# Gated cross-attention with a LoRA mixture: Q of all sixteen head pairs by block products, and two of the seven V products of the first two groups moved to the start

## What is computed

```python
x = _rmsnorm(hidden_states, ln_weight)          # hidden_states: layer norm of the input
h_q = (x @ w_q.T).reshape(b, lq, H, DH)
h_k = (key_value_states @ w_k.T).reshape(b, lk, H, DH)
h_v = (key_value_states @ w_v.T).reshape(b, lk, H, DH)
score = jnp.einsum('bqhd,bkhd->bhqk', h_q, h_k) + position_bias[None]
...
attn = jnp.einsum('bhqk,bkhd->bqhd', softmax(score), h_v).reshape(b, lq, H * DH)
return hidden_states + attn @ w_out.T
```

## Time and profile before

| | us |
|---|---|
| median of 3 runs (lowest, highest) | 823.38 (822.85, 823.48) |
| the profiled execution | 823.18 |
| its span, first to last instruction | 821.4 |
| TensorE busy | 814.2 |
| VectorE busy | 584.1 |
| GpSimd busy | 440.3 |
| ScalarE busy | 385.1 |

### The profile page before, as it was taken

One profiled execution on the slowest core, in us unless ns is written; L12 is line 12 of the kernel. 1 busy time (PEld: TensorE's weight loads), 2 busy tenths in 40 slices (PEclk: granted clock), 3 DMA queues, 4 the chain that ended last, 5 costly groups with the idle time before them and its releaser, 6 DMA issues.

```text
span 821.4 us, 14316 instructions
## 1 busy us (share of the span) xinstructions
PE 814.2 (99%) x4288; PEld 701.3 (85%) x4288; DVE 584.1 (71%) x1003; ACT 385.1 (47%) x1051; POOL 440.3 (54%) x410
## 2 busy tenths in 40 slices
PE   8999999999999999999999999999999999999998
PEld 7888888878888889888888888888888888888887
DVE  6985656767646354987779778877887788778752
ACT  5564444456241514566345634563456355545410
POOL 2366666580476372756764575457545754574200
PEclk9999999999999999999999999999999999999999
DMA  9347445543544555697566556655665565555002
GB/s 305 106 137 259 153 155 171 178 150 127 179 148 160 179 191 163 228 281 234 160 211 230 186 159 211 229 181 163 212 220 180 165 220 210 183 178 180 1 26 78
DMA packets 78991, 145.52 MB, mean 177 GB/s; under 512 B 7920, under 2 KB 45296, under 8 KB 77040
## 3 DMA queue, kind: packets, MB, share of 16 engines
q1 hardware_dynamic: 78960, 145.12, 52.6%
HBM read 94.77 MB, written 50.33 MB: 177 GB/s over the span
## 4 chain that ended last, share of the span: by engine, by line
PE 94%; DVE 2%; issue 1%; DMA 1%; SPq 1%; POOL 1%; ACT 1%; DVEq 0%; POOLq 0%
PE proj_ps L1962 17%; PE proj_ps L1768 15%; PE proj_ps L2018 12%; PE proj_ps L2037 8%; PE score_ps L1768 7%; PE proj_ps L1836 5%; PE score_ps L2037 5%; PE score_ps L1805 3%; PE pv_ps L2037 2%; PE turn_ps L2037 2%; PE proj_ps L2216 2%; PE pv_ps L2018 2%; PE turn_ps L2018 2%; PE turn_ps L1805 2%; PE pv_ps L1805 2%; PE score_ps L1836 2%
## 5 line engine op out<-in xcount | busy, mean ns | idle before, releaser
L618 POOL TENSOR_TENSOR comb<-mask_add,bias_sb 128x1024 f32<-128x1024 f32 x32 | 77.2, 2435 | 144.7 <-DVE attn L1515 144.7
L853 ACT ACTIVATE attn<-attn,neg_max 128x128 f32<-128x128 f32 x256 | 99.2, 391 | 37.4 <-DVE neg_max L1504 37.3
L1064 ACT ACTIVATE w_hi<-w_raw 128x256 fp32r<-128x256 f32 x105 | 39.9, 413 | 96.5 <-POOL w_raw L703 74.2
L713 POOL TENSOR_TENSOR w_lo<-w_raw,w_hi 128x256 fp32r<-128x256 f32 x105 | 74.4, 749 | 0.0
L1537 DVE TENSOR_TENSOR acc<-proj_ps,acc 128x512 f32<-128x512 f32 x70 | 48.3, 690 | 36.4 <-PE proj_ps L1768 36.4
L1768 PE MATMUL proj_ps<-w_hi,tf_hi 128*128 128x512 f32 x156 | 61.1, 391 | 0.0
L1768 PE MATMUL proj_ps<-w_lo,tf_hi 128*128 128x512 f32 x156 | 60.7, 389 | 0.0
L1768 PE MATMUL proj_ps<-w_hi,tf_lo 128*128 128x512 f32 x156 | 60.7, 389 | 0.0
L665 POOL TENSOR_TENSOR w_lo<-w_raw,w_hi 128x256 fp32r<-128x256 f32 x60 | 45.9, 771 | 23.3 <-ACT w_hi L927 23.1
L614 POOL TENSOR_TENSOR w_lo<-w_raw,w_hi 128x1024 fp32r<-128x1024 f32 x20 | 48.3, 2416 | 16.2 <-ACT w_hi L833 16.2
L1384 DVE TENSOR_TENSOR w_lo<-w_raw,w_hi 128x1024 fp32r<-128x1024 f32 (+1 forms) x21 | 27.9, 1345 | 38.0 <-ACT w_hi L964 38.0
(11 more groups left out here) (374 smaller groups left out, 2558.9 us busy)
## 6 DMA issues: line engine op xcount, KB each, us to landing
w_raw<-in_weights SPq DMA_DIRECT2D x50, 512.0 KB, 5.5
v_sb<-v_spill SPq DMA_DIRECT2D x32, 512.0 KB, 3.8
q_spill<-attn SPq DMA_DIRECT2D x60, 256.0 KB, 3.1
qt<-q_spill SPq DMA_DIRECT2D x15, 1024.0 KB, 4.8
block_spill<-block_sb SPq DMA_DIRECT2D x30, 512.0 KB, 3.5
attn<-block_spill SPq DMA_DIRECT2D x120, 128.0 KB, 3.0
w_raw<-in_v_weights SPq DMA_DIRECT2D x12, 512.0 KB, 4.4
v_spill<-v_sb SPq DMA_DIRECT2D x12, 512.0 KB, 5.0
```

Of the source, the lines that this page charges most:

```text
L618: pool.tensor_tensor(comb[:, j, :, :], mask_add[:, :, :], bias_sb[:, j:j + 1, :].to_broadcast([P, B, S]), ALU.add).then_inc(comb_done, 1)
L713: pool.tensor_tensor(columns(w_lo, slot, n), raw, columns(w_hi, slot, n).bitcast(F32), ALU.subtract).then_inc(k_lo, 1)
L853: e = act.activation(probs[:, u, i, :], probs[:, u, i, :], ACT.Exp, bias=neg_max[:, u, i:i + 1], accum_out=row_sum[:, u, i:i + 1])
```

## The change

All 16 pairs of Q are made by block products (`NQ = NPH`), and V in four groups of four pairs, all of 512 columns; pair 0 has no direct product any more except K. Of V's groups 0 and 1, the two products without sums of blocks of the context (0: A11 B11, 2: A12 B21) are made in the head, tile by tile (`early_tile(n, m)`: n = 0, 1 for group 0, n = 2, 3 for group 1), in the order: keys of half 1, early 0 and 1, keys of half 2, four transposes, early 2, two transposes, one tile of early 3, two transposes, three tiles of early 3. Later these groups have five products (`LATE`). Group 1's early tiles use the banks `vy_ps`.

The raw blocks for these come ahead of context half 2 and between the parts of x. ScalarE and VectorE split context half 2 before x's statistics are taken, in ScalarE's case between copies of early tiles. The layer norm of x goes from VectorE to ScalarE (as `x*scale + shift`). Six more warming matmuls run before the keys. Group 0's block R12, formerly read after the last Q phase, is now read within it, by `v_first_sum(3)`; two other sums are made in earlier phases. In the V stage, product 1 is the first. The wait before the scores of a pair is for one addition fewer. The rest of the diff renames semaphores, renumbers counts and moves buffers.

The core of the diff, by engine:

Constants and helpers:

```diff
-NQ = NPH - 1
+NQ = NPH
...
-VPAIRS = ((1, 5), (5, 9), (9, 13), (13, 16))
+VPAIRS = ((0, 4), (4, 8), (8, 12), (12, 16))
...
+VE = 2
+LATE = (1, 4, 3, 5, 6)
...
+        def v_place(g, n):
+
+            return LATE.index(n) if g < VE else n
...
+        v_t = [qt[:, :, :].rearrange("p j (m n) -> p (j m) n", n=HALF) if g == 1 else k_buf[:, :, :] for g in range(VG)]
+        EARLY = (WV, WO, WQ, WV)
```

SyncE:

```diff
+            sp.dma_start(*early_block(0, slice(0, EARLY_HALF))).then_inc(ve_half_in, 16)
+            sp.dma_start(*early_block(0, slice(EARLY_HALF, 2 * EARLY_HALF))).then_inc(ve_in[0], 16)
+            load_early(1)
             for c in range(C):
                 load_ctx(c, 1)
             load_x(0)
-            sp.dma_start(w_raw[:, WV, 0:WN // 2], weights[0, WV][:, 0:WN // 2]).then_inc(wv_half_in, 16)
             load_x(1)
-            sp.dma_start(w_raw[:, WV, WN // 2:WN], weights[0, WV][:, WN // 2:WN]).then_inc(w_in[WV], 16)
+            load_early(2)
             load_x(2)
             load_x(3)
...
+            sp.wait_ge(ve_first_lo, 2)
+            load_early(3)
+            sp.wait_ge(w_lo_done[WK], 1)
+            sp.dma_start(w_raw[:, WK, :], weights[0, WQ]).then_inc(wq_first_in, 16)
...
             sp.wait_ge(qa_lo, NQ * AF)
             sp.wait_ge(s_step, NQ * SF)
-            load_v_block(0, R22)
+            load_v_block(1, R22)
             sp.wait_ge(qs_lo, NQ * SF)
             load_v_block(0, R12)
```

GpSimd:

```diff
+            early_rest(1)
+            early_rest(2)
+            pool.wait_ge(consts_done, 3)
+            inverse_root(1, slice(0, G), 2)
+            pool.wait_ge(xn_done, G)
+            early_rest(3)
+            inverse_root(2, slice(G, B), 2)
```

ScalarE:

```diff
+            def early_copy(n, m):
+
+                g, k = n // 2, n % 2
+                act.wait_ge(ve_prod, n * VTILES + m + 1)
+                if n == 3 and m == 0:
+                    act.wait_ge(v_stored["11"], 32)
+                act.activation((v_t[g], v_11)[k][:, m, :], (vx_ps, vy_ps)[g][m][:, :], ACT.Copy).then_inc(ve_copied, 1)
+
+            def layer(i):
+
+                act.wait_ge(shift_done, i // G + 1)
+                act.activation(acc[:, i, :], acc[:, i, :], ACT.Identity, bias=shift[:, i:i + 1], scale=root[:, 0, i:i + 1]).then_inc(acc_done, 1)
+
+            early_half(0)
+            early_half(1)
+            early_lead(1)
+            copy_proj(0, 0, k_at(0))
+            copy_proj(1, 1, k_at(1))
+            for m in range(VTILES):
+                early_copy(0, m)
+                lead_ctx(m, 1)
+                if m == 2:
+                    early_lead(2)
+            early_copy(1, 0)
+            early_copy(1, 1)
+            early_copy(1, 2)
+            layer(0)
+            early_copy(1, 3)
+            for i in range(1, G):
+                layer(i)
+            early_lead(3)
+            copy_proj(2, 2, k_at(2))
+            copy_proj(3, 3, k_at(3))
...
+            early_copy(2, 0)
+            raw_xt(0)
+            raw_xt(1)
+            early_copy(2, 1)
+            raw_xt(2)
+            raw_xt(3)
+            layer(4)
+            layer(5)
+            early_copy(2, 2)
+            layer(6)
+            layer(7)
+            early_copy(2, 3)
+            lead_xt(4)
+            lead_xt(5)
...
+            act.wait_ge(ve_prod, 3 * VTILES)
+            lead_a(0, 0, 0, 0)
+            lead_a(0, 1, 0, 1)
+            lead_a(0, 2, 1, 1)
+            lead_xt(6)
+            lead_xt(7)
+            lead_t(0)
+            early_copy(3, 0)
+            early_copy(3, 1)
+            act.wait_ge(ve_prod, 2 * VTILES)
             lead_s(0, 0)
...
             lead_t(1)
+            early_copy(3, 2)
             lead_s(0, 1)
+            act.wait_ge(proj_done, UNITS)
+            lead_t(3)
             lead_s(0, 3)
...
+            early_copy(3, 3)
             lead_s(0, 2)
...
             lead_t(2)
```

VectorE:

```diff
-            for c in range(C):
-                rest_ctx(c, 1)
...
+            early_rest_half(0)
+            early_rest_half(1)
...
             first, second = group(0)[0], group(1)[0]
+            for c in range(C):
+                rest_ctx(c, 1)
             x_stats(0)
             ordered(x_stats(1))
             x_variances(0)
-            rest_w(WV, slice(WN // 2, WN), w_hi_done[WV], w_lo_done[WV])
             x_stats(2)
...
+            ordered(x_stats(3))
+            layer_shift(1, first)
...
                 post(i, 5, t_sum, p6_ps[:, :], s_copy)
                 if last:
-                    v_rest(0, 0)
-                    v_first_s1_sum()
+                    v_first_sum(3)
+                    v_rest(0, 1)
...
             ctx_difference(3, 3, first_raw[1], second_raw[1])
+            v_first_sum(4)
```

TensorE:

```diff
+            pe.wait_ge(wk_part_in[0], 16)
+            for _ in range(4):
+                pe.matmul(score_ps[0][:, 0:P], ident[:, :], ident[:, :], start=True, stop=True)
+            pe.wait_ge(wk_part_lo, 1)
+            for _ in range(2):
+                pe.matmul(score_ps[0][:, 0:P], ident[:, :], ident[:, :], start=True, stop=True)
+            first_keys(0)
+            for m in range(VTILES):
+                early_tile(0, m)
+            pe.wait_ge(ve_lo, 1)
+            for m in range(VTILES):
+                early_tile(1, m)
+            first_keys(1)
+            for i in range(G):
+                turn_xn(i)
+            pe.wait_ge(ve_lo, 2)
+            for m in range(VTILES):
+                early_tile(2, m)
             turn_xn(4)
             turn_xn(5)
...
+            pe.wait_ge(ve_lo, 3)
+            early_tile(3, 0)
+            turn_xn(6)
+            turn_xn(7)
+            for m in range(1, VTILES):
+                early_tile(3, m)
...
             def v_group(g):
-                v_product(g, 0, VB["11"], vx_ps, True, posted(g - 1, 13) if g else lambda m: pe.wait_ge(t_done, T_DONE[1]))
+                if g >= VE:
+                    v_product(g, 0, VB["11"], vx_ps, True, posted(g - 1, 13))
...
                 v_product(g, 1, KT1, vy_ps, True, posted(g - 1, 9) if g else stage_a_left)
...
                     if u == 0:
-                        pe.wait_ge(k_post, (a - 1) * KPOSTS + 2)
+                        pe.wait_ge(k_post, (a - 1) * KPOSTS + 1)
```

512 lines of the change are left out of this document (254 added, 258 removed).

## The result

The changed kernel takes 833.04 us (median of 4 runs, 832.13 to 835.08), the kernel before 823.43 beside it: ratio 1.012, 95% interval 1.010 to 1.014. It is 9.6 us slower, where the prediction had 5.9 us and a range up to 832.5. The profiled execution took 835.08 us; all that is read from its trace belongs to that one.

A forecast was written before the change was run, and what follows sets the result against it. TensorE was taken as the bound, busy 814.2 of 821.4 us. Terms +6.5 + 9.5 - 12.9 + 3.1 + 0.3 + 0.2 - 0.8 = +5.9 us gave a median of 829.3 us, range 823 to 832.5.

The forecast's parts named there:

- the head's term: Start to the second Q phase: queue order adds 9.3 us of TensorE waits, so that phase starts 6.5 us later.
- Matmul count, -3.9: Whole kernel: matmuls removed and added on TensorE together save 3.9 us.
- VectorE: 0.7 for the rest of that piece: Head, end of VectorE's split of context half 2 before x's statistics: 0.7 us, ending at 21.4.
- the 0.55 added: Head: the same layout put the earlier kernel's second Q phase at 55.3 instead of 55.84, so 0.55 us was added.
- ScalarE is now the pace: Head, second piece: ScalarE's queue from 28.5 us sets the time; transpose 4 can start at 40.7, a wait of 1.9.
- The joint, +3.1: Q phases to V groups: TensorE waits for VectorE's addition behind the sum reading R12; +3.1 us, bounds 1.3 to 4.
- `v_first_sum(4)`, +0.3: Late Q phases: this sum follows a slow context difference, but VectorE waits for ScalarE there anyway; +0.3 us.
- Group 1's chain +0.2: V stage: loading R11, sums, rests and split end within half a us of TensorE's need; +0.2 us (0 to 1.2).
- scores of pair 1 -0.8: Before the scores of pair 1: the earlier wait goes; -0.8 us (0 to -0.8).
- Rival (c), the clock: Head: the clock falls after waits, 2.7 us more, 832; chance 0.14 together with several small joints adding up.
- (a): Head: TensorE stays the pace and the 9.3 us of waits go; -3.4 us, 820.0 us; chance 0.10.
- (b): Head and joint: nearly even, block 2 lands by 17.5 us and waits shrink; 824.9 us; chance 0.16.

The follow-up runs named there:

- a head without a fall of the clock: Changed kernel with VectorE's second addition of the last Q phase put ahead of the sum that waits for R12; 829.23 us.
- the mended kernel: Changed kernel with VectorE's orders at the V stage and ahead of x, both queues of the first Q phase, and `v_first_sum(4)` moved; 824.17 us.
- filled waits: Changed kernel with identity matmuls put into TensorE's waits at four places, three in the head and one ahead of the V stage; 832.28 us.
- shortened sums: The mended kernel with three VectorE operations of the first Q phase on a quarter of their columns, part of the computation left out; 822.5 us.

## Why the prediction came out as it did

The step that failed is the head's term. It was put at +6.5 us and measured +8.9 in a head without a fall of the clock and +10.3 in the profiled execution. The sum `v_first_sum(4)` (+0.3, measured +1.0) and the clock (nothing in the sum) add the rest.

- **Matmul count, -3.9.** Right. In the trace without waits between (the mended kernel) phases and V stage are what the pitches of the earlier trace rows give, within 0.7 us each.
- **The head, +6.5.** The order of the waits was right: first transpose late for a norm, transpose 4 late for ScalarE's layers, then the T form, then P1's copy. The waits of the head without a fall add up to 8.5 us against the 9.3 predicted. The start of the chain was mis-sized. "VectorE: 0.7 for the rest of that piece" took 2.00, for GpSimd's rest of block 2 beside it; the earlier trace rows held the warning, a 3.42 us operation beside GpSimd, and I used it only for the Q phases. The first transpose came at 31.7 in a head without a fall, instead of 30.9 (with the 0.55 added). Then the first T form waited 2.1 us, not 1.6. From place to place the lateness grows: 0.9 us at the first transpose, 1.1 at transpose 4, 1.8 at the first Q product, 2.3 at the second Q phase (64.71 against 62.4). That GpSimd's rest beside the sum is what was missed is shown by its duration; that leaving it away from there would have saved the time is not, since moved it only fell on another step. My reading "ScalarE is now the pace" was half of it: mending ScalarE's places moved the waits to VectorE, and shortening VectorE alone gave 1.7 us.
- **The joint, +3.1.** Right to a quarter of a us (2.87 from start to start), landing and order each as laid out. The addition comes at 212.67, and TensorE starts 0.15 us after its end.
- **`v_first_sum(4)`, +0.3.** Mis-sized: 1.47 us from start to start against 0.49 before is +1.0. I said that VectorE waits for ScalarE there in any case; that wait was 0.99 us before, the sum takes 1.75, and no wait of VectorE is left.
- **Group 1's chain +0.2, scores of pair 1 -0.8.** No wait shows at the first; the second is gone, and in the profiled execution the last stretch is 1.0 us shorter.
- **Rival (c), the clock.** I gave it 0.14 together with other things; it happened. Behind the V stage's wait a fall costs 1.4 to 1.8 us (V stage 135.8 to 136.1 us in the four traces that have one, 134.3 to 134.5 in nearly all others; 148.73 against 146.96 in the kernel before). In the head, one of the two was swallowed. The profiled execution lost 1.6 + 1.0 us by it, by the comparison with the run that had none; the median run less. By the Trainium skill (TensorE: Matmul & The Clock Gate, "What's actually happening") idle time brings the lower clock; the trace agrees in kind, 0.57 granted from 34 to 38 us behind a wait of 2.46 us. Not every such wait brought it, as told below.

Summed for the median: head chain 2.3, `v_first_sum(4)` 0.7, the clock 0.8 (what filling the waits gave in the runs, itself uncertain by about 1), joint -0.2: 3.6 us, against 3.7 missing. That this comes so near is partly luck: the head's 2.3 is from one trace, and between traces the head's start moves by over 1 us, as told below. Rivals (a) and (b) are out: the waits that they denied are there. That the cost is in places, not in the idea, is shown by the mended kernel; that the idea is worth nothing here too, since its 3.9 us pay for a head that stays 3.2 us longer.

What stays open: runs of one changed kernel spread by 1.4 to 3.7 us where the kernel before spreads by 1.2 to 1.4 in three of the four later comparisons (3.0 in the fourth). The clock's falls don't explain it: in the kernel with the statistics taken ahead the runs with no fall (mean clock 1.000) took 824.2 to 826.0 us and those at 0.998 took 822.8 to 824.2, and in the mended kernel it is 824.9 to 826.1 against 823.4 to 824.3. The traces show two other things that move. ScalarE's split of block 2 starts anywhere from 17.8 to 19.1 us, and in the eight traces with the changed kernel's order up to there the first transpose comes 13.1 us behind it. These are ScalarE's and TensorE's timelines, first of the changed kernel, then of the one with `v_first_sum(4)` moved, which differ in nothing up to here:

```profile
19.06 1.06 ACT L956 ACTIVATE w_hi<-w_raw 128x1024 fp32r<-128x1024 f32 x1 [0.44 <-DMA w_raw<-in_v_weights]
...
17.82 1.06 ACT L956 ACTIVATE w_hi<-w_raw 128x1024 fp32r<-128x1024 f32 x1
...
30.93 0.33 PE L1981 MATMUL score_ps<-ident,comb 128*128 128x128 f32 x1 [2.14 <-DVE comb L1408]
```

In the first the split waits for the block's landing, in the second it does not. And in three traces (filled waits, `v_first_sum(4)` moved, shortened sums) TensorE waits 0.4 to 0.7 us in the K stages for a block read back from DRAM, and the stretch from the first K stage on takes 484.3 to 484.6 us instead of 483.3 to 483.9. No experiment separated these, and one trace per kernel can't tie them to the times of the runs.

## What to carry to other kernels

When work moves into a stage where three engines take turns, count TensorE's matmuls last: lay out the queue of each engine, and price every operation of VectorE twice, alone and beside GpSimd. At a joint, ask which instruction frees the first result bank and what stands ahead of it on its engine; two lines in another order were worth 3.8 us of the 9.6. When an operation of GpSimd is moved out of the way of a long operation of VectorE, look where it lands: beside a step of 0.17 us it cost 1.6. And allow for a fall of the clock behind a new wait of TensorE, unless another wait follows soon enough to swallow it: the shortest wait behind which one was seen here is 1.77 us, and of the 23 waits of 1.75 to 2.00 us in the heads of the traces 8 had one behind them. Where a trace of a variant is set against that of the kernel, compare a point ahead of the edit first: a part of the difference can be there already.

## What the runs showed of the hardware

- Behind a wait of 2.54 to 2.84 us ahead of the V stage the clock fell in four traces of the changed kernel and its variants and stayed up in three. One that stayed up, with VectorE's order ahead of x changed:

```profile
210.52 0.47 PE L2147 MATMUL proj_ps<-w_hi,xt_hi 128*128 128x512 f32 x1 [2.55 <-DVE attn L1487]
210.83 0.40 PE L2147 MATMUL proj_ps<-w_hi,xt_lo 128*128 128x512 f32 x1
```

- A fall need not start with the first matmul behind the wait: in the changed kernel six matmuls start 0.22 to 0.31 us apart, and from the seventh on it is 0.40 to 0.43. In the kernel before with a wait it starts at once.
- VectorE's sum of 512 columns takes 0.69 us alone and 2.00 beside a GpSimd sum of 1024; one of 1024 takes 1.21 alone, 1.75 or 2.83 beside GpSimd; and a step of 8 columns takes 0.17 alone and 1.78 beside one. Moving work from VectorE to GpSimd can lengthen VectorE's queue.
